# A gated cross-attention block with a routed FFN: attended values turned right behind the second score pass and added in the same iteration

## What is computed

```python
x = x + tanh(g_xattn) * attention(layernorm(x), ctx, ctx)      # 16 heads of 16, causal softmax
x = x + tanh(g_ffn) * ffn(layernorm(x))
# ffn: prob = softmax(xf @ w_router + b_router) over 16 blocks; the 4 largest form a 0/1 mask
#      h = relu(xf @ w1.T + b1)      1024 hidden, in 16 blocks of 64
#      y = (h * mask of its block) @ w2.T + b2
```

## Time and profile before

| | us |
|---|---|
| median of 3 runs | 681.58 |
| lowest, highest | 681.28, 682.12 |
| the profiled execution | 680.97 |
| span of its instructions | 679.1 |
| TensorE busy | 659.7 |
| GpSimd busy | 556.0 |
| ScalarE busy | 538.9 |
| VectorE busy | 527.8 |

### The profile page before, as it was taken

One profiled execution on the slowest core, in us unless ns is written; L12 is line 12 of the kernel. 1 busy time (PEld: TensorE's weight loads), 2 busy tenths in 40 slices (PEclk: granted clock), 3 DMA queues, 4 the chain that ended last, 5 costly groups with the idle time before them and its releaser, 6 DMA issues.

```text
span 679.1 us, 30579 instructions
## 1 busy us (share of the span) xinstructions
PE 659.7 (97%) x12960; PEld 611.9 (90%) x12960; DVE 527.8 (78%) x1429; ACT 538.9 (79%) x785; POOL 556.0 (82%) x718
## 2 busy tenths in 40 slices
PE   6779999999999999999999999999999999999997
PEld 5668899999999999999999999989999999999997
DVE  6899887788777778788778878777878877877742
ACT  4668788888888888888888888888888888887732
POOL 6677888988988898888898898888888889887643
PEclk9899999999999999999999999999999999999999
DMA  5323355556545446645556654544554554553110
GB/s 197 96 55 86 88 109 99 116 109 115 120 114 116 99 110 116 111 112 113 100 117 107 116 111 122 103 107 114 113 113 112 116 100 96 98 86 64 28 40 32
DMA packets 192279, 69.24 MB, mean 102 GB/s; under 512 B 166160, under 2 KB 191888, under 8 KB 192144
## 3 DMA queue, kind: packets, MB, share of 16 engines
q1 hardware_dynamic: 191312, 65.72, 45.7%
q10 hardware_dynamic: 832, 1.57, 0.6%
HBM read 19.03 MB, written 8.39 MB: 40 GB/s over the span
## 4 chain that ended last, share of the span: by engine, by line
PE 86%; DVE 5%; DMA 3%; ACT 2%; issue 2%; POOL 1%; SPq 1%; POOLq 0%; DVEq 0%
PE bank L423 11%; PE score_banks L344 10%; PE bank L357 8%; PE score_banks L314 8%; PE bank L425 8%; PE bank L424 8%; PE bank L446 8%; PE bank L447 8%; PE bank L448 8%; PE bank L371 4%; PE bank L401 2%; PE score_banks L327 1%; DMA used_all<-used 1%; PE bank L393 1%; ACT weights L525 1%
## 5 line engine op out<-in xcount | busy, mean ns | idle before, releaser
L880 POOL TENSOR_TENSOR h_low<-hid,h_high 128x512 fp32r<-128x512 f32 x128 | 164.2, 1283 | 12.8 <-ACT hid L560 12.8
L738 DVE SCALAR_TENSOR_TENSOR hid<-bank,b_cols,used_all 128x256 f32<-128x256 f32 x248 | 108.1, 477 | 65.9 <-PE bank L425 58.2
L873 POOL TENSOR_SCALAR_AFFINE_SELECT weights<-weights 128x1024 f32<-128x1024 f32 x128 | 138.2, 1103 | 18.2 <-ACT weights L525 16.4
L423 PE MATMUL bank<-xT_high,w_high 128*128 128x256 f32 x496 | 151.5, 305 | 0.8 <-DVE hid L738 0.7
L525 ACT ACTIVATE weights<-score_banks 128x1024 f32<-128x1024 f32 x128 | 124.3, 1024 | 34.7 <-PE score_banks L344 34.6
L424 PE MATMUL bank<-xT_low,w_high 128*128 128x256 f32 x496 | 139.4, 281 | 0.0
L425 PE MATMUL bank<-xT_high,w_low 128*128 128x256 f32 x496 | 139.4, 281 | 0.0
L446 PE MATMUL bank<-w_high,h_high 128*128 128x256 f32 x488 | 137.3, 281 | 0.7 <-POOL h_low L880 0.7
L447 PE MATMUL bank<-w_low,h_high 128*128 128x256 f32 x488 | 137.7, 282 | 0.0
L448 PE MATMUL bank<-w_high,h_low 128*128 128x256 f32 x488 | 136.2, 279 | 0.0
L423 PEld LDWEIGHTS bank<-xT_high,w_high 128*128 128x128 f32 x496 | 93.3, 188 | 8.9 <-DVE hid L738 1.1
(11 more groups left out here) (105 smaller groups left out, 1411.1 us busy)
## 6 DMA issues: line engine op xcount, KB each, us to landing
x_in<-in_x SPq DMA_DIRECT2D x31, 256.0 KB, 3.1
out_y<-y_out SPq DMA_DIRECT2D x31, 256.0 KB, 2.2
c_in<-in_ctx SPq DMA_DIRECT2D x30, 256.0 KB, 2.8
qT<-qT SPq DMA_DIRECT2D x128, 4.0 KB
w_stage<-in_w1T ACTq DMA_DIRECT2D x1, 1024.0 KB, 9.2
hid<-in_w2T SPq DMA_DIRECT2D x8, 128.0 KB, 2.7
kT_parts<-k_parts SPq DMA_TRANSPOSE x57, 2.8
qT_parts<-q_parts SPq DMA_TRANSPOSE x57, 2.7
```

The costliest lines, as they stand in the source:

```text
L423: pe.matmul(out=bank, lhsT=w1_high[:, k, c], rhs=high, start=k == 0, stop=False)
L738: dve.scalar_tensor_tensor(hid[:, n % 4, j], hid_bank(n)[:, j * TOKS:(j + 1) * TOKS], b1_cols[:, c:c + 1], used_all[:, p % 2], ALU.add, AL ...
L873: pool.affine_select(out=w, in_=w, compare_op=ALU.is_ge, fill=0.0, base=0, pattern=[[0, 2 * HB], [1, S]], channel_multiplier=-1).then_inc( ...
L880: pool.tensor_tensor(h_low[:, p % 2, chunks], hid[:, n % 4], h_high[:, p % 2, chunks].bitcast(F32), ALU.subtract).then_inc(h_low_made, 1)
```

## The change

It reorders all five queues. TensorE turns the attended values behind the second score pass, into bank `M0` from which they came; bank `M1` is left to the router. VectorE's `attention_added` is for tile `i - 1`, in the same iteration. ScalarE's `choice` moves to the start of the next iteration and `hidden_parts(p, m)` ahead of `out_copied`. SyncE's `used_spread` moves behind `max_row`, the loads and the store. The roots for the second LayerNorm are computed one iteration earlier, so the slots of `mv` and `rstd` alternate the other way for it. The early tiles, and the last two, whose `xn` TensorE transposes, do so in iteration `b + 3` in place of `b + 2`. The diff, cut to this:

```diff
@@ TensorE
             def attention_out(b):
...
                 if b >= 1:
-                    pe.wait_ge(att_copied, b)
+                    pe.wait_ge(att_made, b)
...
             def out_transposed(b):
                 s = b % 2
-                pr = router_pair(b + 1)
                 pe.wait_ge(att_copied, b + 1)
-                if pr is not None:
-                    pe.wait_ge(clipped_made, PAIR * (pr + 1))
-                if b >= 1:
-                    pe.wait_ge(att_made, b)
                 for g in range(U):
-                    turned = pe.transpose(banks[M1][:, g * P:(g + 1) * P], ...)
+                    turned = pe.transpose(banks[M0][:, g * P:(g + 1) * P], ...)
...
             def router_logits(p, i):
-                pe.wait_ge(att_made, min(i - 1, N))
+                if p >= 1:
+                    pe.wait_ge(clipped_made, PAIR * p)
...
+                if 0 <= i - 3 < N and x_by_pe(i - 3):
+                    x_transposed(i - 3)
                 if out_b is not None:
                     ffn_out(out_b, 0)
...
                     shifted_scores(i)
-
-                last = i >= N
-                if last and p is not None:
-                    hidden(p, m + 1)
-                if 0 <= i - 2 < N and x_by_pe(i - 2):
-                    x_transposed(i - 2)
+                if 0 <= i - 1 < N:
+                    out_transposed(i - 1)
                 if pr is not None:
                     logits_transposed(pr)
-                if not last and p is not None:
+                if p is not None:
                     hidden(p, m + 1)
                 if out_b is not None:
                     ffn_out(out_b, 1)
-                if 0 <= i - 1 < N:
-                    out_transposed(i - 1)
@@ ScalarE, the loop's body after the change
+                if 0 <= i + 2 < N and q_early(i + 2):
+                    q_evacuated(i + 2)
+                if 0 <= i + 2 < N and k_early(i + 2):
                     k_evacuated(i + 2)
+                if pu is not None:
+                    choice(pu)
+                if last_p is not None:
+                    hidden_parts(last_p, last_m + 1)
+                if not k_early(i + 2) and i + 2 < N:
+                    k_joined(i + 2)
                 weights_high(i)
+                if 0 <= i - 3 < N and x_by_pe(i - 3):
+                    x_copies(i - 3)
                 if 0 <= i - 3 < N and not x_by_pe(i - 3):
                     x_joined(i - 3)
+                if p is not None:
+                    hidden_parts(p, m)
                 if 0 <= i - 1 < N:
                     out_copied(i - 1)
...
                     exponentials(i)
-                if p is not None:
-                    hidden_parts(p, m)
-                if pr is not None:
-                    choice(pr)
                 if QUERIES_BY_PE <= i + 3 < N + MAX_LAG:
                     q_joined(i + 3)
-                if not q_early(i + 3):
-                    rest(i)
@@ VectorE
                     finished(i - OUT_LAG - 1)
+                starting = i < 7
+                if starting and 0 <= i + 1 < N:
+                    row_maximum(i + 1)
                 if 0 <= i - 2 < N:
-                    attention_added(i - 2)
+                    normalised_again(i - 2)
                 if 0 <= i + 3 < N:
                     normalised(i + 3)
-                if 0 <= i + 1 < N:
+                if not starting and 0 <= i + 1 < N:
                     row_maximum(i + 1)
-
-                early = q_early(i)
-                if early and 0 <= i - 2 < N:
-                    normalised_again(i - 2)
                 if p is not None:
                     hidden_masked(p, m)
                 weights_low(i)
-                if not early and 0 <= i - 2 < N:
-                    normalised_again(i - 2)
-                if 0 <= i + 5 < N:
-                    layernorm_stats(i + 5)
+                if 0 <= i - 3 < N:
+                    x_parts(i - 3)
...
+                if 0 <= i - 1 < N:
+                    attention_added(i - 1)
+                if 0 <= i + 5 < N:
+                    layernorm_stats(i + 5)
...
                 if pr is not None:
                     route(pr)
                 if p is not None:
                     hidden_masked(p, m + 1)
@@ GpSimd, the order after the change
   x_split(i - 2); hidden_low(last pair, m + 1); x2 plus bias (i - 2); query_parts; values;
   key_parts; hidden_low(p, m); causal_weights(i); weights_low(i); roots(i), of x_(i + 4) and x2_(i - 1)
@@ SyncE
-                if pu is not None:
-                    used_spread(pu)
                 if 0 <= i < N:
                     max_row(i)
...
                     store(i - OUT_LAG - 1)
+                if pu is not None:
+                    used_spread(pu)
```

More of the change, by code:

```diff
@@ L363, in out_transposed @@
                 s = b % 2
-                pr = router_pair(b + 1)
                 pe.wait_ge(att_copied, b + 1)
-                if pr is not None:
-                    pe.wait_ge(clipped_made, PAIR * (pr + 1))
-                if b >= 1:
-                    pe.wait_ge(att_made, b)
                 for g in range(U):
-                    turned = pe.transpose(banks[M1][:, g * P:(g + 1) * P], oT[:, s, g * S:(g + 1) * S], ident[:])
+                    turned = pe.transpose(banks[M0][:, g * P:(g + 1) * P], oT[:, s, g * S:(g + 1) * S], ident[:])
                 turned.then_inc(att_turned, 1)
@@ L590, in _ @@
                           A_w1T.rearrange("(k p) n -> p k n", p=P)).then_inc(w_landed[0], 16)
-            def rest(i):
-                p, m = hidden_pair(i)
-                if 0 <= i - 2 < N and x_by_pe(i - 2):
-                    x_copies(i - 2)
-                if p is not None:
-                    hidden_parts(p, m + 1)
             for i in ITERATIONS:
@@ L681, in attention_added @@
                 dve.wait_ge(att_turned, b + 1)
-                bank = banks[M1][:].rearrange("p (u r d) -> p u r d", u=U, d=PAD)
+                bank = banks[M0][:].rearrange("p (u r d) -> p u r d", u=U, d=PAD)
                 gains = gain[:, s].rearrange("p (u r) -> p u r", u=U)
@@ L690, in attention_added @@
                     dve.wait_ge(tanh_done, 1)
+                if b >= 2:
+                    dve.wait_ge(x2_b2_made, b - 1)
                 dve.scalar_tensor_tensor(x2[:, s], att[:], tanh_g[:, 0:1], x_in[:, b % XS, :],
@@ L807, in _ @@
                     places(3)
+                if pr is not None:
+                    route(pr)
                 if p is not None:
@@ L910, in _ @@
                 p, m = hidden_pair(i)
-                if 0 <= i + 4 < N or 0 <= i - 2 < N:
-                    if i + 4 == 0:
-                        pool.wait_ge(numbers_set, 1)
-                    roots(i)
+                last_p, last_m = hidden_pair(i - 1)
+                if 0 <= i - 2 < N and not x_by_pe(i - 2):
+                    x_split(i - 2)
+                if last_p is not None:
+                    hidden_low(last_p, last_m + 1)
                 if 0 <= i - 2 < N:
@@ L919, in _ @@
                     pool.tensor_tensor(x2_b2[:, b % GS, :], x2[:, b % 2], gated_b2[:], ALU.add).then_inc(x2_b2_made, 1)
-                last_p, last_m = hidden_pair(i - 1)
-                if last_p is not None:
-                    hidden_low(last_p, last_m + 1)
                 if QUERIES_BY_PE <= i + 3 < N + MAX_LAG:
                     query_parts(i + 3)
-                if 0 <= i - 2 < N and not x_by_pe(i - 2):
-                    x_split(i - 2)
                 if i == FIRST:
@@ L932, in _ @@
                     key_parts(i + 3)
+                if p is not None:
+                    hidden_low(p, m)
                 if 0 <= i < N:
                     causal_weights(i)
-                if p is not None:
-                    hidden_low(p, m)
                 weights_low(i)
+                if 0 <= i + 4 < N or 0 <= i - 1 < N:
+                    if i + 4 == 0:
+                        pool.wait_ge(numbers_set, 1)
+                    roots(i)
                 if i == FIRST + 3:
```

32 lines of the change are left out of this document (8 added, 24 removed).

## The result

The changed kernel takes 749.79 us (median of 5 runs, 748.68 to 755.26); the kernel before took 681.58 beside it (680.99 to 682.12). The ratio is 1.101, 95% interval 1.0972 to 1.1049: slower by a tenth. The profiled execution is the longest of the five, 755.26 us with a span of 753.5, against 680.97 and 679.1.

What follows compares the result with a forecast made beforehand. TensorE bounds the kernel, busy 659.7 of 679.1 us. Span 679.1 + 74 (middle) - 4 (start) + 2 (end) = 751; with 1.9 outside the span 753, and the median 0.6 above: 753.5 us, range 703 to 790.

Steps and rivals of the forecast that it cites:

- Its middle: Odd iterations 9 to 63: 28 times 2.6 us lost, 74 us in all, bounds 32 to 109.
- its end: Last iterations: `used` still stands behind the store, twice; 2 us added, bounds 0 and 4.
- The ladder of the router iteration: VectorE's reciprocal to the next, step by step: 12.46 us against TensorE's 10.03, losing 2.4 us per router iteration.
- I take 3.6, since here too other transfers surround it: SyncE's queue: `used` takes 3.6 us from issue to landing, the median; 2.3 at least, 4.2 at most.
- Rival (1): In the middle `used` lands in 2.3 us: loss 1.1 + 0.2 per pair, total 716; chance 0.2.
- 0.2, near the median's row: VectorE's addition of x beside GpSimd's causal masks: 0.2 us per pair of iterations, bounds 0 to 0.9.
- The clock stays full: TensorE's granted clock: expected to stay full in the changed kernel; no cost given.
- I take 4 us off: Iterations 0 to 6, row maximum first on VectorE: 4 us gained; bounds 9 off and 2 more.
- (b): ScalarE's first FFN split, 1.04 us, ahead of the evacuation of the attended values, which then waits for VectorE's masked evacuation.
- (d): SyncE's queue: `used` behind row-maximum DMAs, loads and store, issued at 5.45 us after the reciprocal; ScalarE's choice in the next iteration.
- The roots on GpSimd: Computed last, ready near 3.3 us after the reciprocal, asked for at 3.7 or 4.9: costed at nothing, up to 0.5.
- The rival on the faster side: Start gains its whole 9 us and the loop costs nothing: 673 us; chance 0.06.

Runs made afterwards that it cites:

- copy-first: Changed kernel with ScalarE's copy of the attended values and router logits ahead of its first FFN split: 710.00 us, ratio 1.0388.
- used-first: Changed kernel with the transpose of `used` back at the front of SyncE's queue: 720.04 us, ratio 1.0538.
- both edits: Changed kernel with `used` at the front of SyncE's queue and ScalarE's copy ahead of the split: 706.34 us, ratio 1.0329.
- the three edits: Changed kernel, ScalarE's copy before the split, search behind the second masked evacuation, `used` behind row-maximum DMAs but ahead of loads and store: 693.11 us.
- the shifted kernel: Changed kernel with 64 small matmuls behind TensorE's warm-up: 777.97 us, ratio 1.1374.
- the choice behind x: The three edits, plus ScalarE's router choice behind the keys and the copies of x in iterations 5 and 7: 694.23 us, ratio 1.0166.
- the filled kernel: Changed kernel with eight identity transposes ahead of those of the attended values in odd iterations from 9: 750.84 us, ratio 1.1001.

## Why the prediction was right, and where it was not

753.5 was forecast and 749.8 measured; for the profiled execution, a span of 751 and 753.5. Its middle was sized at 74 us and took 61.7, its start at -4 and took +11.7, its end at +2 and took +1.0. These are two errors of opposite sign. Within the middle, too, the landing was put too long, the addition too short, and the clock left out. So the mechanism of the middle was right, and the nearness of the total is in part luck.

**What bounds the kernel.** Right: TensorE does the same 12,960 matmuls in nearly the same busy time (673.3 against 659.7 us; six stretches of 3.4 us at half clock are some 10 of the difference), and what is added is its waiting, at the start and, in the middle, in the odd iterations.

**The ladder of the router iteration.** Right in its order, and up to the issue of `used` each rung came some 0.4 us later than forecast. From the reciprocal, forecast against the iteration at 202.45: output tile 4.44 against 4.86; store 4.97 and 5.36; `used` issued 5.45 and 5.85; landed 9.05 and 9.98; evacuation 9.1 and 10.06; transposes turned and next reciprocal 12.46 and 13.34. The last leg, from evacuation to reciprocal, was put at 3.36 and took 3.28. The copy-first and used-first runs show that both edits are needed to close it.

**The landing.** The step "I take 3.6, since here too other transfers surround it" failed. It is 2.3 in 17 of the 27 pairs and 3.3 to 4.1 in ten. Before, it was over 3.2 in 23 of 32, and the median stood for most pairs; after the change 17 of 27 lie far below it, and the mean of the 27 is 2.9. Rival (1) is therefore what most pairs do: 11.16 plus contention was forecast, 11.55 measured. The middle lies between that rival (28 x 1.3 = 36 us) and the forecast (74). The figure of about 2.0 us that the prediction took from the Trainium skill (DMA: Bandwidth & Descriptors, Anatomy of one DMA) was fitted there to DMAs that GpSimd issues. `used` goes out from SyncE's queue; its quick landings here take 2.3.

**Contention.** The step "0.2, near the median's row" was mis-sized. The addition takes 1.10 us in the median, against 0.58, and 0.58 more lies on the loop of each router iteration (from the reciprocal to the statistics of x_in, 274.32 - 271.81 = 2.51, against 1.93). Only the router iteration pays it; the other has room. Over 0.8 us it took in 59 of the 64 tiles, where it had been 11. The rule of the Trainium skill (SBUF — State Buffer, SBUF: two separate sides), that the two engines exclude each other for a whole instruction, was nearer than the row I chose.

**The clock.** "The clock stays full" failed: in the profiled execution it was at half six times in the middle, 9 us. The forecast had TensorE waiting 2.4 us in every second iteration and did not ask what that would do to its clock.

**The start.** "I take 4 us off" failed in sign, and its bounds (9 off, 2 more) did not hold +11.7. It rested on one wait of 0.82 us, read as the cost of a late row maximum. The two experiments on the row maximum show what that move does: put first in the old order, it makes TensorE's transposes of `xn` late and costs 15 us; in the new order it saves 14 that the change would lose, and gives nothing over the kernel before. And the new waits of (b) and (d) in iterations 5 to 8, which I bounded at 2 us, fill the start: tiles 5 to 9 lose 9.5 us in the changed kernel and 4.7 with the three edits. The other 2.4 were there by tile 4, behind the long stretch at half clock.

**Costed at nothing.** The roots on GpSimd: right in this kernel, where no wait for them stands among the larger ones of the middle. With the loop opened (three edits) the second normalisation waits for them, in 120 to 650 us:

```profile
DVE xn L684 <- POOL rstd L813: 22.6, 26, 1.9
```

So the cover was the loop itself. The second masked evacuation behind the search: not named in the forecast at all. It holds TensorE 0.9 us per pair (21.3 us in 24 of them), which I take to be hidden here by the longer loop, and it is most of what is left in the middle once that is opened (pairs of 20.65 with both edits). That the other iteration loses nothing is right: from 283.36 to the next reciprocal it takes 9.98, against 10.03 before.

**The rival on the faster side** fell by its own condition, a masked evacuation 6.1 us after the reciprocal: it started at 8.3 and 10.1, and the start gave nothing.

What stays open: the start of the unprofiled executions; and which wait halves the clock. In the middle of the changed kernel ten waits at the transposes were longer than 1.5 us. Six of them, of 1.67 to 2.33 us, went with a halved clock, and four, of 1.54 to 2.37 us (at 215.1, 327.3, 349.8 and 597.2), did not.

## What to carry to other kernels

Before an instruction is moved ahead on an in-order queue, ask what it waits for, and hand that wait to all that stood behind it, router logits and tiny DMAs included. Of a duration with two clusters take each cluster for itself; its median belongs to the old alignment and may fit no pair of the new one. And a wait seen once at the start is no price for it: write down the loop there too, since putting one engine's producer first makes another producer late.

## What the runs showed of the hardware that was not expected

**A small DMA lands late where a packet of instructions is fetched.** These are the queues' packets in two windows of the changed kernel that begin at an issue of `used` (packets, MB, share of the DMA engines). The first, 208.3 to 210.6:

```profile
q1 hardware_dynamic: 542, 0.32, 47.5%
q8 instruction: 1, 0.02, 4.0%
...
used_all<-used SPq DMA_TRANSPOSE x1, 4.1
```

The second, 186.7 to 189.2:

```profile
q1 hardware_dynamic: 560, 0.33, 44.1%
...
used_all<-used SPq DMA_TRANSPOSE x1, 2.3
```

A packet of 16 KB of the instruction queue begins 1.5 us after the first issue, and the next one to the second 2.8 us after it. In the profiles of before, after, the filled and the shifted kernel every landing of `used` over 3.2 us has such a packet beginning between 0.4 us before and 2.2 us after the issue, and every landing of 2.3 us has none there. It isn't so in all versions: with the three edits and with the choice behind x, eight quick landings have a packet that begins 0.1 to 0.4 us before the issue. What is shown is that they go together, not by which path.

Which pairs are hit seems to follow TensorE's count of instructions. The page of before and after has 102 packets, 1.67 MB, on this queue, and 2 x 12,960 instructions on TensorE: one packet for some 254. In the changed kernel the slow landings come back about every 5.6 pairs (pairs 2, 7 and 8, 12 to 14, 18 and 19, 24 and 25, 30, and pair 0 too). If each pair uses a whole number of packets and 1/5.6 = 0.18 of one more, then 16 more instructions in a pair (the filled kernel: 8 weight loads and 8 matmuls) make that 0.18 + 16/254 = 0.24, and they should come back every 4.2 pairs. They do: pairs 2, 6, 10, 14 and 15, 18 and 19, 22 and 23, 27, and past the regular ones 29. (By the profile a quick pair has 404 matmuls and 403 loads, 3.18 packets of 254.) That the slow pairs of the filled kernel are others, while its loads and stores kept their places in the program, speaks against the traffic of these as the cause. The shifted kernel had 256 more at its start, one whole packet (103 in place of 102), and its slow pairs kept their places, for this or for another reason. I worked this out after the runs, so it is an estimate that fits two of them and no forecast that was tested. In the kernel before the landing cost nothing; the change put it on the path.

**An addition beside the causal masks.** Beside GpSimd's causal masks, where 63 of the 64 additions of two SBUF operands now lie, one takes 1.10 us in the median. It was 0.58 before, beside GpSimd's other work for the most part, and 0.48 with nothing beside it.
